# Four cross-attention layers on one core: PSUM pairs taken in turn in the grouped layer, the last layer's bias built in turned slots, and a new order on POOL

## The reference, cut to what matters

```python
q, k, v = x @ Wq, ctx @ Wk, ctx @ Wv
logits = einsum('bhqd,bhkd->bhqk', q, k) * 64 ** -0.5 + col_bias   # tokens A and B pushed down by 20
x = softmax(logits) @ v @ Wo + bo + x
```

## Time and profile before

| | us |
|---|---|
| median of 3 runs (lowest to highest) | 3557.74 (3557.01 to 3557.79) |
| the profiled execution's own time | 3557.41 |
| its span, first to last instruction | 3555.5 |
| an ordinary turned slot | 30.14 |
| a grouped slot with a bias matrix (43) | 27.69 |

### The profile page before, as it was taken

How to read it: one execution, slowest core, us unless ns; L and a number is a source line. 1 busy time by engine, 2 the same in 40 slices (tenths; PEclk the granted TensorE clock), 3 DMA queues, 4 the chain that set the end, 5 groups by cost and what they waited for, 6 DMA issues and landing times.

```text
span 3555.5 us, 70138 instructions
## 1 busy us (share of the span) xinstructions
PE 3391.0 (95%) x27432; PEld 1541.2 (43%) x27432; DVE 2337.7 (66%) x4440; ACT 1758.3 (49%) x2230; POOL 2198.9 (62%) x1057
## 2 busy tenths in 40 slices
PE   5999999999997888889999999999999999999997
PEld 2444444444432322234444444444444444444442
DVE  6666666666666788846666666666566666666663
ACT  3444444444445677754444444444444444444443
POOL 4877777767641000128776777777787767767776
PEclk8999999999998999999999999999999999999998
DMA  4000000000000000000000000000000000000000
GB/s 142 10 10 10 1 10 10 10 1 9 6 10 11 8 12 17 17 1 10 10 9 3 10 10 3 8 10 10 1 10 10 9 3 10 10 1 10 3 1 24
DMA packets 50161, 42.09 MB, mean 12 GB/s; under 512 B 4912, under 2 KB 42160, under 8 KB 49840
## 3 DMA queue, kind: packets, MB, share of 16 engines
q1 hardware_dynamic: 49840, 37.62, 3.5%
HBM read 32.36 MB, written 2.10 MB: 10 GB/s over the span
## 4 chain that ended last, share of the span: by engine, by line
PE 89%; ACT 3%; DVE 3%; issue 2%; POOL 2%; SPq 0%; DMA 0%; POOLq 0%; ACTq 0%; DVEq 0%
PE ps_j L802 39%; PE ps_j L991 19%; PE ps_st L951 13%; PE ps_sm L885 6%; PE ps_st L936 3%; PE ps_j L978 3%; ACT pt L1323 2%; PE ps_sm L965 2%; PE ps_j L1011 1%; PE ps_st L885 1%; POOL acc L683 1%; PE ps_j L894 1%; PE ps_j L1027 0%; PE ps_j L1002 0%; PE ps_st L914 0%
## 5 line engine op out<-in xcount | busy, mean ns | idle before, releaser
L683 POOL TENSOR_TENSOR acc<-acc,pt 128x1024 f32<-128x1024 f32 x576 | 1380.1, 2396 | 576.9 <-ACT pt L1323 534.2
L1323 ACT ACTIVATE pt<-ps_st 128x1024 f32<-128x1024 f32 x768 | 742.8, 1019 | 551.1 <-PE ps_st L951 532.1
L991 PE MATMUL ps_j<-pt,v 128*64 128x512 f32 x3072 | 704.8, 601 | 3.0 <-DVE q_l L1601 1.3
L1696 DVE CUSTOM_DVE_ANT_0 ps_sm<-ps_sm,bias_m,nmx 128x512 f32<-128x512 f32 x668 | 481.7, 757 | 277.4 <-PE ps_j L885 225.9
L802 PE MATMUL ps_j<-w_h,ctx_h 128*128 128x128 f16 x3072 | 532.3, 220 | 1.5 <-ACT bias_m L1403 1.1
L802 PE MATMUL ps_j<-w_l,ctx_h 128*128 128x128 f16 x3072 | 531.2, 219 | 0.0
L802 PE MATMUL ps_j<-w_h,ctx_l 128*128 128x128 f16 x3072 | 531.2, 219 | 0.0
L1696 DVE CUSTOM_DVE_ANT_0 ps_sm<-ps_sm,bias_m 128x512 f32<-128x512 f32 x492 | 338.5, 707 | 184.1 <-PE ps_j L885 163.2
L991 PEld LDWEIGHTS ps_j<-pt,v 128*64 128x64 f32 x3072 | 205.1, 137 | 416.2 <-issue 374.3
L704 POOL TENSOR_TENSOR o_un<-o_un,rinv 128x512 f32<-128x512 f32 x112 | 142.1, 1269 | 381.8 <-ACT rinv L1335 299.7
L1733 DVE RECIPROCAL rinv<-rinv 128x256 f32<-128x256 f32 x192 | 334.3, 1745 | 19.8 <-ACT rinv L1339 10.4
(11 more groups left out here) (161 smaller groups left out, 5301.0 us busy)
## 6 DMA issues: line engine op xcount, KB each, us to landing
w_raw<-wk SPq DMA_DIRECT2D x25, 256.0 KB, 2.7
pt<-ctx_t SPq DMA_DIRECT2D x6, 1024.0 KB, 7.7
w_raw<-wv SPq DMA_DIRECT2D x24, 256.0 KB, 3.7
wo_raw<-wo SPq DMA_DIRECT2D x28, 128.0 KB, 2.0
w_raw<-wq SPq DMA_DIRECT2D x24, 128.0 KB, 2.9
k_h<-k_l SPq DMA_DIRECT2D x72, 32.0 KB, 2.0
x<-x_t SPq DMA_DIRECT2D x4, 512.0 KB, 8.2
acc<-ctx_t SPq DMA_DIRECT2D x2, 1024.0 KB, 8.1
```

The costliest lines, as they stand in the source:

```text
L683: G.tensor_tensor(total, first, pt[:, n % RING, :], ALU.add).then_inc(s_acc, 1)
L991: last = MM(dst[h * HD:(h + 1) * HD, :], values_of(p)[:, kt, h * HD:(h + 1) * HD], pt[:, (units(p) + kt) % RING, h * TQ:(h + 1) * TQ], sta ...
L1323: A(pt[:, n % RING, :], src.rearrange("p h q -> p (h q)"), ACT.Exp).then_inc(s_exp, 1)
L1696: last = V.tensor_tensor_reduce(out=src, in0=src, in1=bias_m[:, t, half * HALF:(half + 1) * HALF], scale=-1.0, scalar=nmx[:, 0, t, h:h + 1 ...
```

## The change

In the grouped layer maxima and scores take turns in three pairs of banks: `pair_users()` lists them in TensorE's order, the n-th gets pair n mod 3 (both pairs of `ps_st`, then `ps_sm`), and `take_pair` waits until the user three before has been read, by VectorE for maxima and by ScalarE for scores. In slots with keys to project (32, 33, 46, 47: `keyed`) projections, sums and reciprocals move by one step, and the sums go to bank 0. The first grouped slot gets an order of its own: the value projections of task 33 start before its first maxima, its mean squares before the sums, output projections go from steps 7 and 8 to 9 and 10, key projections from 8 and 9 to 5 and 6. Slots 78 and 79 become turned slots; each of their four blocks builds one bias matrix in the second bank of `ps_sm`, between the extra rows and the maxima, and the second maxima unit waits for its copy. On POOL, `split_x` is parted: xh goes ahead of `sums_lo`, xl stays behind, and the bo sums go between `add(s, 5)` and `add(s, 6)`.

```diff
+def block_bias(s, i):
+    first = STARTS[3] - 2
+    return 16 + 4 * (s - first) + i if first <= s < first + 2 else None
 def turned(s):
-    return 0 <= s < N and not grouped(s) and not G0 - 3 <= s < G0 and s - STARTS[3] not in (-2, -1)
+    return 0 <= s < N and not grouped(s) and not G0 - 3 <= s < G0
+def pair_users():
+    users = [("max", G0, u) for u in range(KT, 2 * KT)]
+    for s in range(G0, G1):
+        last = s == G1 - 1
+        for i in range(20 if last else 16):
+            if not last:
+                users.append(("max", s + 1, i))
+            elif i < 16 and i % 2 == 0:
+                users.append(("max", s + 1, i // 2))
+            if i >= 4:
+                users.append(("st", s, i - 4))
+            elif s > G0:
+                users.append(("st", s - 1, 12 + i))
+    return users
+        def pair(kind, p, u):
+            n = turn_of[kind, p, u] % 3
+            return ps_st[:, n] if n < 2 else ps_sm[:]
+            def take_pair(kind, p, u):
+                n = turn_of[kind, p, u]
+                if n >= 3:
+                    before, q, v = turns[n - 3]
+                    pe.wait_ge(s_max if before == "max" else s_exp, units(q) + v + 1)
+                elif n == 2:
+                    pe.wait_ge(s_max, units(G0) + KT)
+                else:
+                    pe.wait_ge(s_exp, units(G0))
...
                 if summing:
-                    for kt in range(5, KT):
-                        add(s, kt)
+                    add(s, 5)
                     if s - STARTS[layer_of(s)] < B:
                         add_bo(layer_of(s), batch_of(s))
+                    add(s, 6)
+                    add(s, 7)
...
                 def score_block(i):
                     extra_scores(s, i)
-                    for p, u in next(places):
+                    opening, n = next(places), block_bias(s, i)
+                    if n is not None:
+                        p, u = opening[0]
+                        pe.wait_ge(s_max, units(p) + u)
+                        bias_matrix(n)
+                    for p, u in opening:
                         maxima(p, u)
                     turned_scores(s, i)
+                    if n is not None:
+                        pe.wait_ge(s_bias_sb, n + 1)
```

More of the change, by code:

```diff
@@ L486, in build @@
         order = bank_users()
+        turns = pair_users()
+        turn_of = {user: n for n, user in enumerate(turns)}
         place = {(kind, p): bank for kind, p, bank in order}
@@ L497, in values_of, with bias_in @@
             return v32[:, b if grouped(p) else p % 2]
+        def pair(kind, p, u):
+            n = turn_of[kind, p, u] % 3
+            return ps_st[:, n] if n < 2 else ps_sm[:]
         def maxima_in(p, u):
-            late = G0 < p <= G1 or p == G0 and u >= KT
-            return ps_st[:, u % 2] if late else ps_sm[:]
+            return pair("max", p, u) if ("max", p, u) in turn_of else ps_sm[:]
+        def bias_in(n):
+            return bank("bias", n) if n < 16 else ps_sm[:, 1]
         def heads_in(p, u):
@@ L956, in group_scores @@
                 kt, tile, r = j // 2, j % 2, p % 3
[L957 to L960, removed]
+                take_pair("st", p, j)
+                dst = pair("st", p, j)
                 if j < 2:
@@ L1402, in bias_out @@
                     act.wait_ge(s_max, units(STARTS[3] - 1) + n % 8 + 1)
-                A(bias_m[:, t, half * HALF:(half + 1) * HALF], bank("bias", n), ACT.Copy).then_inc(s_bias_sb, 1)
+                A(bias_m[:, t, half * HALF:(half + 1) * HALF], bias_in(n), ACT.Copy).then_inc(s_bias_sb, 1)
             context_hi(0)
@@ L1411, in wide_slot @@
                 now, nxt, far, past = 0 <= s < N, 0 <= s + 1 < N, 0 <= s + 2 < N, 0 <= s - 1 < N
-                def bias(gap, after):
-                    if last_bias(s, gap, after) is not None:
-                        bias_out(last_bias(s, gap, after))
                 def context(*parts):
@@ L1550, in group_slot @@
                         exponentials(s, i - 4)
-                    elif not first:
+                    else:
                         exponentials(s - 1, 12 + i)
@@ L1560, in group_slot @@
                         normed_hi(rms_batch(s))
-                    if i == 7 and not first and has_values(s + 2):
-                        keys_hi(s + 2, 0)
-                    if i == 11 and first:
-                        squares(rms_batch(s + 1))
-                    if i == 10:
+                    if i == 10 + keyed:
                         if has_values(s + 1) and not last:
@@ L1882, in group_slot @@
                     both_halves(s)
+                keyed = has_values(s + 2)
                 for i in range(16):
+                    if first:
+                        if i == 2:
+                            group_rows(s, 0)
+                            group_rows(s, 1)
+                        if i == 8:
+                            keys_lo(s + 2, 1)
+                        if i == 13:
+                            queries_lo(s + 2)
+                        if i == 15:
+                            queries_lo(s + 2, 1)
+                        maxima(s + 1, i)
+                        if i in (4, 5):
+                            reciprocal(s - 1, i - 4)
+                        if i == 8:
+                            normed(rms_batch(s))
+                        if i in (10, 11):
+                            add_out(s - 1, i - 10)
+                        continue
                     if i in (3, 4):
                         group_rows(s, i - 3)
-                    if i == 10 and has_values(s + 2):
+                    if i == 6 and keyed:
+                        keys_lo(s + 2, 0)
+                    if i == 9 and keyed:
                         keys_lo(s + 2, 1)
-                    if i == 12:
+                    if i == 12 + keyed:
                         queries_lo(s + 2)
-                    if i == 14 and grouped(s + 2):
+                    if i == 14 + keyed and grouped(s + 2):
                         queries_lo(s + 2, 1)
@@ L1903, in group_slot @@
                         wo_lo(set_of(s - 1))
-                    if i in (7, 8) and first:
-                        add_out(s - 1, i - 7)
-                    if i == 7 and not first:
-                        if has_values(s + 2):
-                            keys_lo(s + 2, 0)
+                    if i == 7:
                         reciprocal_by_query(s - 1)
```

231 lines of the change are left out of this document (127 added, 104 removed).

## The result

The changed kernel takes 3550.26 us (median; 3547.89 to 3555.58 in 15 runs). The kernel before, run beside it, takes 3558.12 (3556.81 to 3566.93). The ratio is 0.9973, 95% interval 0.9965 to 0.9981: 7.9 us faster. The forecast was 3545.5 us, with a range of 3526 to 3564. The profiled execution took 3552.7 us, 2.4 above the median, with a span of 3550.8 where before had 3555.5.

What follows compares the result with a forecast made beforehand. TensorE, busy 95% of the span, was taken as the bound, with waits in the grouped layer. Terms 24.3 - 9.4 - 8.3 - 18.6 = -12.0 on the profiled 3557.4 us gave 3545.5 us as median; range 3526 to 3564.

Steps and rivals of the forecast that it cites:

- Turns in the grouped layer: Slots 34 to 45: scores now wait for VectorE's reduction of the step before; +2.3 us per plain slot, +24.3 in sum.
- S(13): Score pair of grouped step 13 (M: maxima pair); claimed 1.04 us late, waiting for VectorE's reduction of step 12.
- The query split ahead of the reduction: Grouped slots, steps 12 and 14: VectorE splits the query projection before reducing maxima, making the next score 1.04 us late.
- R1: Rival: turns free the grouped layer, slots 34 to 45 lose about 2.6 us each, total 3490 us; chance 0.08.
- Exit: Slots 46 and 47: waits before sums and reciprocals go, some lateness is given back; net -9.4 us, bounds -12 and -4.
- Entry: Slots 32 and 33: waits go and clock recovers, against later scores held by VectorE; -8.3 us, bounds -20 and +2.
- Outside the layer: Slots 1, 49 and 77 to 81: moved bias matrices and POOL's new order save 18.6 us, bounds -8 and -22.
- R2: Rival, half price: lateness in grouped slots is absorbed in later steps, +1.1 us a slot, total 3533 us; chance 0.15.
- R4: Rival: bias copies are late and POOL's delay moves to the sums, about +10 us, total 3556 us; chance 0.10.
- (d): Layer 3's eight bias matrices move to the small banks, copies hidden under score matmuls; price at most 3.1 us in all.
- (e): POOL's new order: xh cast earlier, bo sums ahead of add 6; xl finished about 2.1 us earlier.
- R3: Rival, the clock: one fall to 1.2 GHz in every late slot, 1.7 us each, 12 times, total 3566 us; chance 0.12.

Runs made afterwards that it cites:

- e2_old_banks: The changed kernel without the turns: scores back in one pair of banks, maxima in two, everything else kept; 3530.24 us.
- e3_turns_only: The kernel before with only the grouped layer's turns added, maxima ahead of scores; 3582.56 us.
- e5_split_behind: The changed kernel with VectorE's query splits moved behind the reduction of their step, in slots 34 to 45 that project no keys; 3535.85 us.
- e4_scores_first: The changed kernel with the score pair issued ahead of the maxima pair in each grouped step, in code and table of turns; 3522.91 us.
- e7_entry_swapped: The changed kernel with scores ahead of maxima in the first grouped slot (32) alone; 3546.32 us.
- e1_wide: The kernel before with only the edits outside the grouped layer: slots 78 and 79 turned, bias matrices moved, POOL's new order; 3542.08 us.
- e6_pool_only: The kernel before with POOL's (GpSimd's) new order alone; 3550.04 us.
- e8_out_later: The kernel with scores first in all grouped slots, one output projection moved from step 0 to step 1, not in slots 37, 41, 45; 3518.51 us.

## Why the prediction was right, and where its terms were not

It was right in sign, in size within 4.8 us, and in the place of the loss. By its terms:

- **Turns in the grouped layer**: +24.3 forecast, +22.0 by the windows, +20.0 on the medians (e2_old_banks to changed), +24.4 with what they do in entry and exit (e3_turns_only, whose slots 34 to 45 give +18.8). A plain slot loses 1.85, not 2.33. The step that was mis-sized is "TensorE goes on 0.15 after its end (1429.91 to 1430.05)": that row names a DMA as releaser, not the reduction. In the changed kernel the reduction ends at 1453.59 + 1.21 = 1454.80 and the score starts at 1454.86: 0.06, so 0.09 less. S(13) would have stood 0.23 behind its M(13), at 1453.92, and is 0.94 late where 1.04 was forecast. The forecast's walk from S(6) on can be laid beside the two traces: S(10) was taken 0.20 early and is 0.24 early, S(13) 0.85 late and is 0.70, S(15) 1.88 and is 1.65, S(2) 1.89 and is 1.55, the next S(6) 2.34 and is 1.85. The error grows by 0.04 to 0.15 from point to point, which fits 0.09 too much at each of the slot's five waits (0.45 of 0.48); that this is the whole of it is argued, not shown.
- **The query split ahead of the reduction** as the cause: shown by e5_split_behind, which moves nothing else, for 1.20 of the 1.85 of a slot. The rest stands at S(2), S(4) and S(6), where nothing was moved: there it is argued from the waits alone. e4_scores_first takes these waits away too, but brings others.
- **R1, the turns free the layer**: fell on three sides (e2_old_banks, e3_turns_only and the changed kernel). But e4_scores_first shows what it needed: the same three pairs, taken in the other order, remove 20.8 us of waits and bring 19.0.
- **Exit**: -9.4 forecast, -7.2 measured. The waits of the earlier trace rows are gone, but the turns leave 3.6 us of waits for nmg there, where the forecast gave back 2.3. Without the turns it is -6.0 (e2_old_banks), and the turns alone are +2.9 (e3_turns_only, slot 46 at a clock of 0.91): these do not add up to -7.2, and why was not settled.
- **Entry**: -8.3 forecast, -1.0 measured, the largest error. The new order alone gives -4.1 (148.9 in e2_old_banks), the turns alone +3.9 (e3_turns_only), together -1.0: they add up to -0.2, as near as this stage can tell. The waits that were to go went (4.1 for GpSimd is 0.4). Two terms were mis-sized. The scores' hold on VectorE was taken at 2.7 to 4 in each of two slots and the query splits; slots 31 to 33 have 14.6 us of it, of which the one at 1087.64 is 3.3. And the clock was to win back half or all of some 10 us of TensorE's work, but the clock of slot 32 rose only from 0.80 to 0.82 and TensorE's busy time in slots 31 to 33 fell by 1.1 (122.05 to 120.94). In e7_entry_swapped, with 6.4 us of those waits, it is 115.77.
- **Outside the layer**: -18.6 forecast. The windows give -1.6 (slot 1), -3.1 (slot 49) and -11.4 (slots 77 to 81), 16.1 in all, and e1_wide 16.1 on the medians. Slot 1 was taken at twice its worth: without the clock's fall it has still a wait, 32.48 for 30.14. Slots 77 to 81 were -12.3 in the forecast; slot 77 takes 30.35, and slots 78 to 81 take 30.8 to 31.6, not 30.1 to 30.5.
- **R2 and R4** are out with these: lateness is not absorbed at half price, and the reorders of (d) and (e) pay 8 us each (e6_pool_only, e1_wide).
- **R3, the clock**: eight of the twelve slots, seven of them at a clock of 1.00 and one at 0.99, lose 1.85 to 2.2; slots 36, 40 and 44 have 0.94, 0.95 and 0.91, where before had 1.00, 0.94 and 1.00 (the 1.00 over slots 34 to 45 on which the forecast's "the trace does not bear it out yet" rests is a mean that hides the 0.94 of slot 40). So a part of it is real: in slot 44 the changed kernel takes 32.77 and e3_turns_only, at 1.00 and with the same steps there, 31.25. That the falls do not follow the code alone is seen in e7_entry_swapped, whose slot 36 has 1.00 with the same steps and waits; what starts one was not settled. "TensorE: Matmul & The Clock Gate" of the Trainium skill, section "A second HAM failure mode: psum-queue depth-cycling", reports such swings in a kernel that cycles through PSUM banks with small idles between its groups of matmuls. No run here parts that from other reasons; e8_out_later, with fewer waits, has 0.91 in slot 36 as well.

The sum: entry 7.3, outer slots 2.5 and exit 2.2 us were taken too good, the turns 2.3 too dear, 9.7 together. The four terms make -2.3 by the windows, for the -12.0 forecast. The two profiled executions differ by 4.7: the start and the end, named in no term, gave the other 2.4. The medians differ by 7.9, since the changed kernel's profiled execution lies 2.4 above its median. That the total came within 4.8 us, with terms 9.7 off, was partly luck: 5.6 of the 7.9 us measured came from what no term covered. Two small slips of the prediction change nothing: 3557.7 less 12.0 is 3545.7, not 3545.5, and a slot's idle is 2.67, not 2.65.

## What to carry to other kernels

When buffers are handed round among users, write down for each user which engine frees the one it takes, and what stands ahead of that on its queue: three pairs in place of two and one cost 20.0 us with maxima ahead of scores (3530.2 to 3550.3), and with scores ahead the same three gave 7.3 us over the old banks (3530.2 to 3522.9). Here a split that waits for another engine belonged behind the reduction that TensorE is about to need; moving two of them a slot was worth 14.4 us, a part of it the clock's. Time edits of one change apart: here one of them alone, GpSimd's order, gave as much as all together.

## What the runs showed of the hardware

- In slot 43 of the changed kernel TensorE starts 0.06 us after the end of the VectorE reduction that frees its bank (1454.80 to 1454.86).
- Slots of different kernels with the same steps can agree to 0.01 us when the clock is 1.00 (slot 43: 27.69 in before and e2_old_banks; 29.54 in the changed kernel and e3_turns_only). Within one kernel they need not: in e4_scores_first slots 39, 41, 42, 43 and 45, alike in their steps and all at a clock of 1.00, take 27.43 to 27.55.
- The granted clock of a slot with the same steps and the same waits differs from kernel to kernel (slot 36: 0.94 in the changed kernel, 1.00 in e7_entry_swapped, 30.92 against 29.65 us), though TensorE had done the same, to 0.02 us, in the slot up to the fall. In slots 34 to 45 of the ten traces the falls are in slots 36, 40 and 44, those with weight splits (the slot behind one shows 0.98 or 0.99 at times); which of the three has one differs. The changed kernel's own runs spread over 7.7 us; that this is the reason was not shown.
